# Numbering the extra expert tiles of a token-sorted layer in two halves

## The reference

```
affinity = sigmoid(x @ centroids.T)            # 16 experts
_, top_idx = top_k(affinity + gate_bias, 2)
weights = top_aff / (top_aff.sum(-1) + 1e-9)
for e in range(16):
    routed += mask[..., e:e+1] * swiglu(x, wg[e], wu[e], wd[e])
return 0.1 * swiglu(x, wg_s, wu_s, wd_s) + routed
```

## Time and profile before

| | |
|---|---|
| median of 3 runs | 1204.17 us (1201.83 to 1209.49) |
| profiled execution | 1201.35 us |
| its span in the trace | 1200.1 us |
| mean granted TensorE clock | 0.906 |
| PE busy | 984.1 us (82%) |
| DVE, ACT, POOL busy | 751.6, 633.8, 526.0 us |
| the first sorted layer (layer 1), scatter to first expert tile | 382.46 to 406.69 us |
| the second (layer 3) | 1096.71 to 1130.32 us |

### The profile page before, as it was taken

One profiled execution on the slowest core, in us unless ns is written; L12 is line 12 of the kernel. 1 busy time (PEld: TensorE's weight loads), 2 busy tenths in 40 slices (PEclk: granted clock), 3 DMA queues, 4 the chain that ended last, 5 costly groups with the idle time before them and its releaser, 6 DMA issues. The chain is left out here.

```text
span 1200.1 us, 17877 instructions
## 1 busy us (share of the span) xinstructions
PE 984.1 (82%) x5740; PEld 783.3 (65%) x5740; DVE 751.6 (63%) x1969; ACT 633.8 (53%) x1824; POOL 526.0 (44%) x582
## 2 busy tenths in 40 slices
PE   4947897177997592679999999999999889987794
PEld 2534454035586372668988888888888768676583
DVE  3775222165665236878888888788877588765243
ACT  1532343102124154689797878888878654652252
POOL 1422476344552462344545554444543145443253
PEclk8879899688997795689999999999999899998797
DMA  9120698703001575101101010101000061005674
GB/s 391 41 72 26 161 217 196 165 0 103 1 1 62 189 255 202 40 11 48 58 1 58 2 57 2 58 2 58 1 23 2 1 217 27 1 15 187 197 254 154
DMA packets 61550, 106.66 MB, mean 89 GB/s; under 512 B 13872, under 2 KB 42320, under 8 KB 59792
## 3 DMA queue, kind: packets, MB, share of 16 engines
q1 hardware_dynamic: 52208, 87.51, 22.6%
q0 software_dynamic: 9248, 18.00, 6.0%
HBM read 78.14 MB, written 26.27 MB: 87 GB/s over the span
## 5 line engine op out<-in xcount | busy, mean ns | idle before, releaser
L2825 POOL TENSOR_TENSOR a_p<-a_p,a_tot 128x128 f32<-128x128 f32 x64 | 51.0, 816 | 206.1 <-DVE a_tot L2437 206.1
L200 PE MATMUL bank<-a_w_high,a_in 128*128 128x128 f32 (+1 forms) x512 | 125.8, 287 | 6.3 <-DVE a_in L2037 4.7
L200 PE MATMUL bank<-a_w_low,a_in 128*128 128x128 f32 (+1 forms) x512 | 121.8, 284 | 0.0
L200 PEld LDWEIGHTS bank<-a_w_high,a_in 128*128 128x128 f32 x512 | 100.4, 196 | 8.4 <-issue 4.6
L200 PEld LDWEIGHTS bank<-a_w_low,a_in 128*128 128x128 f32 x512 | 100.6, 196 | 0.0
L1995 POOL DMA_INDIRECT f_ys<-f_y,f_got x54 | 51.8, 960 | 64.1 <-ACT f_y L1966 59.5
L2488 DVE TENSOR_REDUCE a_top<-bank 128x2 f32<-128x512 f32 (+1 forms) x96 | 56.9, 602 | 32.2 <-PE bank L2290 19.7
L2659 ACT ACTIVATE a_qn<-bank,a_q_shift,a_q_rstd 128x128 f32<-128x128 f32 x128 | 48.3, 460 | 41.4 <-POOL a_q_shift L256 41.4
L1821 DVE SCALAR_TENSOR_TENSOR f_swi_inner<-bank,f_swi_gated 128x128 f32<-128x128 f32 x78 | 22.6, 291 | 74.1 <-ACT f_swi_gated L1036 49.6
L2466 DVE TENSOR_SCALAR a_qn<-bank,a_qk_minus,a_qk_rstd 128x128 f32<-128x128 f32 x192 | 64.1, 406 | 6.6 <-POOL a_qk_rstd L253 4.2
L1036 ACT ACTIVATE f_swi_gated<-bank 128x128 f32<-128x128 f32 x78 | 21.6, 277 | 86.6 <-PE bank L200 67.1
(11 more groups left out here) (413 smaller groups left out, 2974.0 us busy)
## 6 DMA issues: line engine op xcount, KB each, us to landing
expert<-in_experts SPq DMA_DIRECT2D x49, 384.0 KB
f_expert<-in_experts SPq DMA_DIRECT2D x31, 384.0 KB, 6.1
third_shelf<-in_groups SPq DMA_DIRECT2D x8, 1024.0 KB, 6.4
f_got<-f_xs SPq DMA_DIRECT2D x10, 516.0 KB, 6.9
f_got<-f_ys SPq DMA_DIRECT2D x16, 256.0 KB, 4.1
third_shelf<-in_groups SPq DMA_DIRECT2D x8, 512.0 KB, 4.2
f_xs<-blank_zero SPq DMA_DIRECT2D x1, 3999.0 KB, 21.7
l_expert<-in_experts SPq DMA_DIRECT2D x10, 384.0 KB
```

The lines of the kernel that those rows point to most:

```text
L200: ins = pe.matmul(out, lhs, rhs, start=start and n == 0, stop=stop and n == len(pairs) - 1, skip_group_check=shared)
L2825: g_.tensor_tensor(cross_probs(m, ti), cross_probs(m, ti), over(m.tot[n % 2][:, first:first + HPG], SC), ALU.mult).then_inc(*s["cross_weig ...
```

## The change

The slots are worked out in two passes, one for each half of the tokens (`slots_vector(…, half)`). The extra tiles that the first half's counts open are given out first; those that only the second half opens are numbered behind all of the first half's. So the slots of tiles 0 to 3 no longer depend on the second half's counts. POOL waits for its rows and slots tile by tile.

```diff
 def sparse_ffn_tensor
-    if not p.weighed_rows:
+    if p.weighed_rows:
+        ranks(0)
+    else:
         logits_tensor(k, p, s4, 0)
...
     logits_tensor(k, p, s4, 1)
-    ranks(0)
+    if not p.weighed_rows:
+        ranks(0)
     for r in range(2):
         open_shared(r)
     ranks(1)
+def slots_vector(k, p, m, s, half):
...
+    on.wait_ge(*s["ranked"].at(half + 1))
+    rank = bank[5][:, half * HALF * p.routed:(half + 1) * HALF * p.routed].rearrange("p (t e) -> p t e", e=p.routed)
...
+    if half:
+        v.tensor_tensor(opened, opened, m.opened[0][:], ALU.subtract).then_inc(*step.one())
+        on.wait_ge(*step.now())
...
+    if half:
+        v.tensor_tensor(m.far[:], rank, under(m.limit[:], HALF), ALU.is_ge)
+        v.scalar_tensor_tensor(m.later[:], base, m.end[0][:, p.routed - 1:p.routed], m.end[0][:], ALU.add,
+                               ALU.subtract).then_inc(*step.one())
+        on.wait_ge(*step.now())
+        v.scalar_tensor_tensor(m.far[:], m.far[:], float(P), under(m.later[:], HALF), ALU.mult, ALU.mult)
+    else:
+        v.scalar_tensor_tensor(m.jump[:], base, float(P), m.first[:], ALU.mult, ALU.add).then_inc(*step.one())
...
+    if half:
+        v.tensor_tensor(place, place, m.far[:], ALU.add).then_inc(*step.one())
...
+    v.tensor_copy(m.slot[:, tiles, :], slot_f).then_inc(*s["slots_ready"].one())
+    if half == 0:
+        v.tensor_tensor(m.end[0][:], base, opened, ALU.add)
+        v.tensor_scalar(m.limit[:], opened, float(P), float(P), ALU.mult, ALU.add).then_inc(*step.one())
 def sparse_ffn_vector
     if p.weighed_rows:
...
         norm_rows_vector(k, s4, 1, k.x, m.rows)
+        slots_vector(k, p, m, s, 0)
+        limit_vector(k, p, m, s4, 1)
     else:
...
         weights_vector(k, p, m, s4, 0)
-    limit_vector(k, p, m, s4, 1)
+        limit_vector(k, p, m, s4, 1)
+        slots_vector(k, p, m, s, 0)
     choose_vector(k, p, m, s4, 1, facts)
...
-    on.wait_ge(*s["ranked"].at(2))
...
+    slots_vector(k, p, m, s, 1)
     inner(2, p.share)
 def sparse_ffn_pool
-    for r in rows_of(s4):
-        on.wait_ge(*r[0])
     on.wait_ge(*m.blank)
-    on.wait_ge(*s["slots_ready"].at(1))
     rows = bass.IndirectOffsetOnAxis
     for i in range(NT):
+        for r in rows_of(s4)[i]:
+            on.wait_ge(*r)
+        on.wait_ge(*s["slots_ready"].at(i // HALF + 1))
```

More of the change, by code:

```diff
@@ L1501, in sparse_routing @@
     m.lower = sb("lower", [P, e, e])
+    m.in_front = sb("in_front", [P, e, e])
     return m
@@ L1559, in sparse_ffn @@
         m.over = sb("over", [P, p.routed, HALF * TPB - 1])
-        m.tiles = sb("tiles", [P, p.routed])
-        m.base = sb("base", [P, p.routed])
+        m.opened = [sb(f"opened{n}", [P, p.routed]) for n in range(NT // HALF)]
+        m.base = [sb(f"base{n}", [P, p.routed]) for n in range(NT // HALF)]
+        m.end = [sb(f"end{n}", [P, p.routed]) for n in range(NT // HALF)]
+        m.limit = sb("limit", [P, p.routed])
         m.jump = sb("jump", [P, p.routed])
+        m.later = sb("later", [P, p.routed])
         m.place = sb("place", [P, NT, p.routed])
+        m.far = sb("far", [P, HALF, p.routed])
         m.slot_f = sb("slot_f", [P, NT, TOP])
         m.slot = sb("slot", [P, NT, TOP], U32)
-        m.passed = sb("passed", [P, MORE, p.routed])
+        m.passed = [sb(f"passed{n}", [P, MORE, p.routed]) for n in range(NT // HALF)]
+        m.owner_of = [sb(f"owner_of{n}", [P, MORE]) for n in range(NT // HALF)]
         m.owner_f = sb("owner_f", [P, MORE])
@@ L1839, in sparse_ffn_vector @@
     inner(1, p.share)
-    on.wait_ge(*s["ranked"].at(2))
[L1842 to L1855, removed]
-    v.tensor_tensor(m.place[:], m.place[:], rank, ALU.add).then_inc(*step.one())
-    on.wait_ge(*step.now())
-    v.tensor_tensor(m.chosen[:], m.hits[:], by_choice(m.place[:]), ALU.mult).then_inc(*step.one())
-    on.wait_ge(*step.now())
-    v.tensor_reduce(m.slot_f[:], m.chosen[:], AX.X, ALU.add).then_inc(*step.one())
-    on.wait_ge(*step.now())
-    v.scalar_tensor_tensor(m.slot_f[:], m.where_f[:, :, 0:TOP], float(P), m.slot_f[:], ALU.mult, ALU.add).then_inc(
-        *step.one())
-    on.wait_ge(*step.now())
-    v.tensor_copy(m.slot[:], m.slot_f[:]).then_inc(*s["slots_ready"].one())
+    slots_vector(k, p, m, s, 1)
     inner(2, p.share)
@@ L1868, in sparse_ffn_vector @@
         weights_vector(k, p, m, s4, 1)
-    v.tensor_tensor(m.base[:], m.base[:], m.tiles[:], ALU.add).then_inc(*step.one())
+    v.scalar_tensor_tensor(m.end[1][:], m.base[1][:], m.end[0][:, p.routed - 1:p.routed], m.opened[1][:], ALU.add,
+                           ALU.add).then_inc(*step.one())
     on.wait_ge(*step.now())
-    v.tensor_tensor(m.passed[:], under(m.base[:], MORE), over(iota[:, 0:MORE], p.routed), ALU.is_le).then_inc(*step.one())
+    for n in range(NT // HALF):
+        ins = v.tensor_tensor(m.passed[n][:], under(m.end[n][:], MORE), over(iota[:, 0:MORE], p.routed), ALU.is_le)
+    ins.then_inc(*step.one())
     on.wait_ge(*step.now())
-    v.tensor_reduce(m.owner_f[:], m.passed[:], AX.X, ALU.add).then_inc(*step.one())
+    for n in range(NT // HALF):
+        ins = v.tensor_reduce(m.owner_of[n][:], m.passed[n][:], AX.X, ALU.add)
+    ins.then_inc(*step.one())
+    on.wait_ge(*step.now())
+    v.scalar_tensor_tensor(m.owner_f[:], m.owner_of[0][:], float(p.routed), m.owner_of[0][:], ALU.is_lt,
+                           ALU.mult).then_inc(*step.one())
+    on.wait_ge(*step.now())
+    v.tensor_tensor(m.owner_f[:], m.owner_f[:], m.owner_of[1][:], ALU.add).then_inc(*step.one())
     on.wait_ge(*step.now())
```

28 lines of the change are left out of this document (27 added, 1 removed).

## The result

| | before | changed |
|---|---|---|
| median, 20 runs each | 1204.23 us | 1196.47 us |
| lowest to highest | 1200.92 to 1212.49 | 1189.58 to 1205.36 |
| ratio, 95% interval | | 0.993 (0.9911 to 0.9949) |
| profiled execution, its span | 1201.35, 1200.1 us | 1205.36, 1204.1 us |

The changed kernel is 8.4 us faster by the ratio (6.1 to 10.7), which is under 1%. Its profiled execution was the slowest of its 20, so absolute times of the two traces can't be subtracted. I read each sorted layer from a point that both kernels pass before the change acts: the start of `f_logits` of the first half in layer 1 (359.7 before, 363.9 after) and of the second half in layer 3 (1087.5 and 1092.1).

A forecast was written before the change was run, and what follows sets the result against it. Layer 1 was taken as bound by slots, 16 scatter issues and fetch, layer 3 by the shared expert. -9.5 + 2.5 = -7.0 us gave 1194.4 from the profiled execution, 1197.2 from the median; 1196 was taken, range 1187 to 1204.

The forecast's parts named there:

- Layer 1, -9.5 us: Layer 1's slots, scatter, fetch and first tile: last scatter issue at 392.1 for 401.72, gain 9.5 us.
- late signals: PE's results reach others late from about 8 us after the first scatter to its end; price in layer 3 9.7 us.
- DVE's second half: Layer 1's second-half slot chain: starts at 378.70, 15 instructions for 11, costs 0.6 us more, slots at 382.05.
- The bound of 7.0: Layer 1's gain if late signals last through the second half and delay the shared expert: 2.5 us of 9.5 lost.
- Layer 3, +2.5 us: Layer 3's net loss: DVE reaches inner(3) 5.0 us later, part given back by late signals; bounds +5.3 and -4.7.
- The working up to `inner(3)`: DVE's added work in layer 3: 3.3 us first half, 0.4 second half, 1.2 owner; inner(3) 5.0 us later.
- what late signals give back: In layer 3, the earlier scatter end lets PE recover part of the 5.0 us delay, leaving +2.5 us.
- the 8 us after the first issue: Layer 3's late signals start about 8 us after the first scatter, at 1100, before PE gets inner(3) at 1103.5.
- counting steps among them: Layer 3: PE enters late signals with 5 fast steps fewer done, leaves 4.3 us sooner: +2.9 or +1.5 us.
- Rival 1: Late signals leave PE alone in layer 3: -14.2 us, 1187 to 1190 us; chance 0.20.
- Rival 2: Idle PE in layer 3 drops to clock 0.50 and stays there: +8.8 us, 1210 to 1213 us; chance 0.08.
- Rivals 3 and 4: Halves don't part, 1205 to 1208 us, chance 0.05; DVE locks POOL out, 1199 to 1201 us, chance 0.04.

The follow-up runs named there:

- layer 3 only: Changed kernel with only layer 3 given out in two halves, layer 1 as in the kernel before: 1206.16 us, ratio 0.9997 to the kernel before.
- layer 1 only: Changed kernel with only layer 1 given out in two halves, layer 3 as in the kernel before: 1197.31 us, ratio 0.993 to the kernel before.
- the third set: Session on another chip: kernel before unchanged (1190.13 us), changed kernel unchanged (1181.53), and changed kernel with layer 3's owners after inner(5) (1175.31).
- the first set: Session of four runs on one chip (kernel before 1205.49 us): one layer split at a time, then layer 3's scatter withheld (1220.65) or paused (1205.27).
- owner late, paced: Changed kernel with layer 3's owners after inner(5) and its scatter in groups of 6, 6 and 4 issues: 1181.92 us, ratio 0.9925.
- owner late: Changed kernel with layer 3's owner chain moved behind inner(5), against the changed kernel: 1179.43 us, ratio 0.9914; again 1175.31 and 1176.72 us.

## Why the prediction was right, point by point

The forecast was 1196 us for 1196.47, with -7.0 us for about -8.4. That it came so close is in part luck: its two terms were off in opposite directions, at the first tiles the gain of layer 1 by 1.4 us too large and the loss of layer 3 by 2.3 us too large, and the 1196 was a choice between 1194.4 and 1197.2. The mechanism of layer 1 was right; in layer 3 the size of one term was not.

- **Layer 1, -9.5 us.** Measured -8.1 at the first tile and -9.0 at the first write; without late signals -10.1 and -10.0. The change's own part was sized well: `slot` of the first half, first issue (10.9 relative for the 11.4 forecast) and spacing. The step that was off is DVE's second half. I had slots at 382.05, 22.3 relative; they were written by 24.0, since late signals struck DVE's chain, which I had only read as PE's trouble: its 15 instructions took 5.06 us for the 3.35 forecast, and 3.20 for the changed kernel where signals are in time. Those 1.7 us are most of the shortfall. From slots to last issue POOL then took 9.6 us for 10.05, which made up a little; that its first issue came 0.4 us early did not, since it waited for the second half's slots anyway. The bound of 7.0, for late signals on the shared expert, had its reason too: PE ended its shared steps only when the rows had come.
- **Layer 3, +2.5 us.** The working up to `inner(3)` held: mask +3.15 for +3.3, `inner(3)` +4.65 for +5.0, last issue -4.5 for -4.3. The term that failed is what late signals give back: taken as 2.5, it was 4.4. Two steps behind it failed. I had PE among late signals from `inner(3)` at 1103.5 to about 1114.5, by the 8 us after the first issue; in the changed kernel the first one came 13.1 us after it, at 1109.79, and layer 3 only has the same (two traces; why, no run shows). And counting steps among them left out what follows them. Behind the last issue the kernel before has 6 gated tiles to go, two of them some 3 us behind the one ahead at the half clock, and the changed one 10, the last eight 1.41 to 1.48 us apart: 14.5 us and 19.2 us to the first tile, 4.8 more, from a last issue 4.5 earlier. Where there are no late signals, the first tile was 2.3 us late, near my number for another reason (the scatter bounded the kernel before, the shared expert the changed one).
- **Rival 1**, late signals leave PE alone, didn't happen on the first chips; on the others they are absent altogether, from both kernels, and there the change gains 10 us, not 14.
- **Rival 2**, PE's clock in layer 3: the steps after 1123 ran 1.41 us apart, at full clock. The clock did decide something where signals are in time, on the other side: ahead of the tiles, where the kernel before idles.
- **Rivals 3 and 4**: the halves parted, and POOL was not held up. All of the scatters in the changed kernel:

```profile
L2041 POOL DMA_INDIRECT f_xs<-f_wide,f_slot x32: 956/960/1105, 374.9 to 1115.9; - x32
```

About half of them now run beside DVE's gating and slots, and the median is 960 ns for 963. The Trainium skill (SBUF — State Buffer, SBUF: two separate sides) warns of a lock-out of GpSimd's descriptor writes by VectorE; these instructions show none. No run here shows it for other forms of DVE work.

Split by layer, the runs say it directly: layer 1 alone gives 8.4 us, as much as the whole, and layer 3 alone nothing that can be told from none. The stages add up as well: -8.96 + 0.24 = -8.7 us at the first writes for 8.4 measured, and on the other chip -10.02 + 0.28 = -9.7 for 10.1. The changed kernel's trace was longer by 4.2 us ahead of layer 1 and by 9.3 from its first write to layer 3's starting point. Neither is the change's: layer 1 only, with the same layer 1, takes as long behind its first write as the kernel before (672.7 and 672.9 us). About half of the 9.3 is PE's clock in the attention ahead of layer 3. From 26.8 to 16.6 us ahead of the starting point it was at its lower level in eight of the fourteen traces, kernels with and without the change, and at full in the other six. The same stretch in the two traces of the changed kernel, the second from the third set:

```profile
1065.30:1075.50 10.20, 9.96 (x40) 9.05 (x40) 5.31 (x18) 3.16 (x6) 2.54 (x7) 0.50 0.00 0
```

```profile
1048.40:1058.60 10.20, 8.81 (x67) 7.90 (x66) 7.69 (x24) 5.68 (x11) 6.41 (x12) 1.00 0.00 0
```

The first comes out 4.8 us later. So a single execution can lose or gain, elsewhere, more than half of what the change is worth.

A version that may be better still is the changed kernel with the `owner` chain behind `inner(5)` in layer 3: 0.9878 to 0.9915 of the kernel before on three chips, where the changed kernel has 0.9915 on the one where both ran. There its first tile is 3.5 us earlier, and its median 1175.31 for 1181.53 us. But the intervals of the two ratios overlap, and all of this is without late signals.

## What to carry to other kernels

Work that is given out earlier gains only up to the next input of its first consumer, so work out where that one stands: in layer 1 it left 8 to 10 us, in layer 3 nothing. The instructions that do it must not stand ahead of the chain that is critical; a part of them moved back brought the first tile 3.5 us forward where nothing else hid them. And measure between anchors within the stage, and on more than one chip, before a stall is called the kernel's.

## What the runs showed of the hardware that I had not expected

- **Late signals belong to some chips, or to their sessions.** While POOL issues indirect DMAs 1.22 to 1.27 us apart, PE's semaphores are raised up to 7 us behind its matmuls (the longest, 7.3 us, in layer 1 of layer 3 only), and DVE waits up to 0.85 us for its own last instruction, in the two traces of the result and on the chip of the first set; on three other chips no semaphore of PE is over 0.6 us late. They begin mostly 7 to 9 us after the first issue, but 13.1 us in the changed kernel's layer 3, and 5.6 us after a pause of 3.8 in its layer 1. On the first set's chip, pauses of 2 us between groups of four issues ended them, one of 0.9 us did not (one trace). In layer 3 they cost the kernel before 9.6 us at the first tile (42.8 for 33.1) and 7.7 at the first write, by one trace each. Their cause is open.
- **A short wait can cost more than its length.** In layer 1, after an idle time of 3.4 us, PE ran its next 29 matmuls at a mean clock of 0.63, in 8.26 us; after one of 2.0 us at 1.00, in 5.68 us (its two levels are 0.50 and 1.00, 1.2 and 2.4 GHz). After 3.9 us ahead of layer 3's first tile, in the kernel before without late signals, it was 0.59, which is why a first tile 2.3 us earlier there was worth 0.3. After one of 2.4 us in layer 3 (owner late, paced) the clock was 0.76, and the stretch to the first write took 7.06 us for 5.8 in owner late, where PE had not idled. The last wait does not decide it alone: in layer 1 only it was 0.42 us, but one of 3.6 us stood 2.8 us ahead of it, and the clock was 0.68, the stretch 7.74 us.
